# VectorE's plan and result steps reordered, and the second expert layer done one half of the rows at a time

## The chip, the cores and the metric

One core of a Trainium2 chip runs the whole kernel. The metric is device time in microseconds, the median of several executions: 927.52 us before (926.98 to 929.14).

## The reference

A gated cross-attention layer and a mixture of experts, on x of 4 x 1024 tokens of width 256:

```python
x = x + tanh(g_xattn) * attention(ctx_768, layernorm(x), ...)
xf = layernorm(x)
probs = softmax(xf @ w_router)              # 8 experts
topk_w, topk_idx = top_k(probs, 2)
h = gelu(einsum('te,ieh->tih', xf, w1) + b1)     # hidden 1024
out = einsum('tih,ihe->tie', h, w2) + b2
x = x + tanh(g_ffn) * sum(out * weights[..., None], axis=1)
```

## The kernel before

The engines' programs are written out by hand, one block each (`block.sync`, `gpsimd`, `scalar`, `vector`, `tensor`), and meet at semaphores. Up to about 479 us the kernel does the attention of the four sequences; beside it the router chooses two experts for every token, and each token's normed row, with its number and its weight, is scattered to the region of its expert in a table `routed` in memory. Behind that the expert stage runs over tiles of TM = 256 rows of one expert. Of a tile, two halves of 128 rows (m = 0, 1; MH = 2) become output partitions. Tiles 0 to 8 (KTILES = 9) belong to three experts with three tiles each, known beforehand (their first rows come from the first sequences); the last sequence's router work is done beside them. From tile 9 on, `plan_tiles` works out from the counts which rows, and which expert, each tile has; a run-time loop does these (`Fori`). In this data there are 35 tiles.

One tile goes so. SyncE loads its rows (`load_rows`, L547) into `lnf`. TensorE turns them (`turn_tile`, L1828), ScalarE and VectorE split them in a high and a low part (`turned_hi` L876, `turned_lo` L1277), since each product is done as three (high by high, low by high, high by low). TensorE does the first layer (`first_layer`, products at L1664, 48 of them, in eight chunks c of the hidden 1024), ScalarE the gelu per chunk (`hidden`, L884), VectorE the split of its outputs per pair of chunks, the quarters q = 0 to 3 (`activate`, L1302 and L1304, semaphore `g_ready`). TensorE turns the next tile's rows between its two layers, and does the second layer (`second_layer`, L1860, 48 products): for q, for m, six products into psY[m]; psY[0] is in psF, psY[1] in psO. Behind the last quarter `expert_done` is raised for each m. VectorE (`results`, L1317 to L1325) adds b2, takes the token numbers (`token_i`), multiplies by the tokens' weights, and raises `result_ready`; GpSimd (`add_rows`, L694) adds both halves to the output in memory by indirect DMAs, whose landing is `added`. `move_meta` (L1309) and `take_meta` (L1281) carry numbers and weights of the tile along.

When the next tile has another expert, VectorE cuts w1 (L1286, after ScalarE's L872, in `change_first`) behind `take_meta`, does `results`, copies b2 (`new_bias`, L1295) and cuts w2. The cut of w1 raises `w1_ready`, for which SyncE waits before it loads the next expert's w1 and, behind it in its queue, the rows of the tile after the next. When the expert stays, `keep_expert` raises `w1_ready` and `w2_ready` without work; TensorE's first layer waits for it.

The order of VectorE at the end of a tile is: four times `activate`, `move_meta`, `turned_lo` of the next tile, `take_meta`, then `keep_expert` and `results`. Three tiles have more: in tile 3 `router_logits` of the last sequence and in tile 4 its `router_slots` stand ahead of `keep_expert`, in tile 6 `plan_tiles`:

```python
else:
    if t == 6:
        plan_tiles()
    keep_expert()
    results(t)
```

SyncE loads the rows of tile 9 once all scatters have landed and the plan is there. GpSimd's queue at this place holds the adds of tile 4, six scatters, the adds of tile 5, six scatters, the adds of tile 6, four scatters, the adds of tile 7.

## Time and profile before

| | |
|---|---|
| median of 3 runs | 927.52 us |
| the profiled execution | 927.44 us, of which 925.5 us are the span |
| TensorE products busy | 857.1 us, 93% |
| VectorE busy | 645.4 us, 70% |
| ScalarE busy | 514.2 us, 56% |
| GpSimd busy | 332.1 us, 36% |
| granted TensorE clock | 0.9 or more in all 40 slices but two at 0.8 |
| chain that ended last | TensorE 55%, issue 14%, VectorE 11%, GpSimd 10% |

Times are from the start of the span. PE is TensorE's products, PEld its loads of weights (the stationary operand), DVE VectorE, ACT ScalarE, POOL GpSimd, and SPq the queue of SyncE, which issues DMAs. A row of the order of time gives start, duration, engine, line, operation and tiles, and in brackets how long the engine was idle before and what ended that. Of TensorE's products the ends are modelled and overlap the next one's start; their rhythm is told by the starts.

### The profile page before, as it was taken

To read this page: it belongs to the slowest core of one execution; us is meant where nothing else is said; L and a number is where in the kernel's file an instruction comes from. 1 tells how busy PE (TensorE), PEld (TensorE's weight loads), DVE (VectorE), ACT (ScalarE), POOL (GpSimd) and SP (SyncE) were. 2 spreads that over 40 slices of the span, in tenths; PEclk is the share of its full clock that TensorE was granted. 3 is DMA by queue.
4 is the path that set the end of the run, shared out by engine and by line. 5 is a ranking of instruction groups with operands and counts; after the bars stand their busy time and mean duration, and the time that the engine had idled before them with its cause. 6 is when DMAs were issued, how large, how long until landed. Compare 5 with 4: busy or idle time off the path is not lost.

```text
span 925.5 us, 19447 instructions
## 1 busy us (share of the span) xinstructions
PE 857.1 (93%) x5968; PEld 657.7 (71%) x5968; DVE 645.4 (70%) x1500; ACT 514.2 (56%) x1371; POOL 332.1 (36%) x241
## 2 busy tenths in 40 slices
PE   3898899999999999998989999899999999999995
PEld 3654445544455454554449999899999999999995
DVE  6767766677766767667786778675765776575685
ACT  2668775787766877558742645243433443353462
POOL 2333223332376323662153227532232223232233
PEclk9999999999999999999999999899999999999998
DMA  4801000120012201120034449352343526352272
GB/s 125 242 1 49 1 1 1 46 94 1 2 58 80 92 1 46 58 92 1 1 109 116 114 105 268 82 138 45 74 107 47 136 37 150 46 140 47 34 221 31
DMA packets 71899, 70.31 MB, mean 76 GB/s; under 512 B 18593, under 2 KB 66977, under 8 KB 71841
## 3 DMA queue, kind: packets, MB, share of 16 engines
q1 hardware_dynamic: 57696, 52.73, 19.2%
q0 software_dynamic: 13152, 16.86, 10.5%
q8 instruction: 30, 0.49, 0.2%
q14 instruction: 29, 0.23, 0.1%
q10 hardware_dynamic: 992, 0.00, 0.1%
HBM read 44.04 MB, written 26.31 MB: 76 GB/s over the span
## 4 chain that ended last, share of the span: by engine, by line
PE 55%; issue 14%; DVE 11%; POOL 10%; ACT 5%; DMA 3%; DVEq 0%; POOLq 0%; SPq 0%; ACTq 0%
PE psS L1664 22%; PE psF L1860 10%; PE psO L1860 10%; POOL rr L676 6%; PE psO L1797 4%; POOL routed L686 4%; PE psS L1781 3%; DVE p_sum L1134 3%; PE psF L1664 2%; DMA out<-V,token_i 2%; PE psF L1828 2%; ACT sq L823 1%; ACT p_ring L867 1%; DMA xr<-in_x 1%; DVE qkd L1108 1%
## 5 line engine op out<-in xcount | busy, mean ns | idle before, releaser
L884 ACT ACTIVATE V<-psS,b_col 128x256 f32<-128x256 f32 x280 | 117.1, 471 | 216.2 <-PE psS L1664 205.4
L694 POOL DMA_INDIRECT out<-V,token_i x70 | 120.4, 1720 | 271.8 <-DVE V L1325 246.4
L676 POOL TENSOR_TENSOR rr<-ssm,minus_half 128x4 f32<-128x4 f32 (+1 forms) x72 | 119.9, 1665 | 254.3 <-DVE ssm L1098 254.1
L867 ACT ACTIVATE p_ring<-psS,shift 128x1024 f32<-128x1024 f32 x128 | 136.5, 1112 | 71.9 <-PE psS L1781 71.6
L1797 PE MATMUL psO<-p_ring,V 128*64 128x512 f32 x576 | 148.5, 612 | 1.5 <-ACT o_sb L855 1.5
L1134 DVE TENSOR_TENSOR p_sum<-p_sum,p_ring 128x1024 f32<-128x1024 f32 (+1 forms) x112 | 136.0, 1215 | 0.6
L1860 PE MATMUL psF<-ln_hi,K 128*128 128x256 f32 x560 | 123.3, 284 | 0.2 <-DVE K L1304 0.2
L1781 PE MATMUL psS<-Q,K 64*128 64x512 f32 x864 | 120.2, 409 | 0.6 <-ACT p_ring L867 0.5
L1860 PE MATMUL psO<-ln_hi,K 128*128 128x256 f32 x560 | 120.2, 278 | 0.0
L1781 PEld LDWEIGHTS psS<-Q,K 64*128 64x128 f32 x864 | 75.9, 184 | 61.0 <-issue 42.7
L1304 DVE TENSOR_TENSOR K<-V,K 128x512 fp32r<-128x512 f32 x140 | 97.1, 694 | 4.8
L1302 DVE CAST K<-V 128x512 fp32r<-128x512 f32 x140 | 60.2, 430 | 51.7 <-ACT V L884 51.3
L1860 PEld LDWEIGHTS psF<-ln_hi,K 128*128 128x128 f32 x560 | 95.1, 188 | 0.8 <-issue 0.4
L1860 PEld LDWEIGHTS psO<-ln_hi,K 128*128 128x128 f32 x560 | 95.0, 188 | 0.0
L1664 PE MATMUL psS<-w_hi 128*128 128x256 f32 x280 | 81.2, 290 | 8.2 <-issue 8.2
L1664 PE MATMUL psS<-w_lo,w_hi 128*128 128x256 f32 x280 | 80.7, 288 | 0.0
L1664 PE MATMUL psS<-w_hi,w_lo 128*128 128x256 f32 x280 | 80.6, 288 | 0.0
L1664 PE MATMUL psS<-w_hi,wc_hi 128*128 128x256 f32 x280 | 79.3, 283 | 0.0
L1664 PE MATMUL psS<-w_lo,wc_hi 128*128 128x256 f32 x280 | 79.2, 283 | 0.0
L1664 PE MATMUL psS<-w_hi,wc_lo 128*128 128x256 f32 x280 | 79.2, 283 | 0.0
L1860 PE MATMUL psO<-ln_lo,K 128*128 128x256 f32 x280 | 78.0, 278 | 0.5 <-issue 0.5
L1860 PE MATMUL psF<-ln_lo,K 128*128 128x256 f32 x280 | 77.9, 278 | 0.0
(289 smaller groups left out, 1764.0 us busy)
## 6 DMA issues: line engine op xcount, KB each, us to landing
xr<-in_L_ffn_w SPq DMA_DIRECT2D x11, 1024.0 KB, 7.9
xn<-in_L_ffn_w SPq DMA_DIRECT2D x11, 1024.0 KB, 5.3
lnf<-routed SPq DMA_DIRECT2D x35, 258.0 KB
routed<-pad_rows SPq DMA_DIRECT2D x17, 258.0 KB, 9.5
xr<-in_x SPq DMA_DIRECT2D x8, 512.0 KB, 4.4
xb<-in_x SPq DMA_DIRECT2D x4, 1024.0 KB, 5.9
out<-xb SPq DMA_DIRECT2D x4, 1024.0 KB
b_raw<-in_L_ffn_b SPq DMA_DIRECT2D x11, 128.0 KB, 3.4
```

Of the source, the lines that this page charges most:

```text
L676: pool.tensor_tensor(rr[0:p, c % 2, n], ssm[0:p, c % 2, n], minus_half[0:p, n], ALU.pow).then_inc(rr_ready, 1)
L686: pool.indirect_dma_start(routed, bass.IndirectOffsetOnAxis(ap=slot_i[:, k, t:t + 1], axis=0), rows_of(b)[k][:, t, :], None, bounds_check= ...
L694: pool.indirect_dma_start(out_rows, bass.IndirectOffsetOnAxis(ap=token_i[:, m:m + 1], axis=0), y_out[:, m, :], None, bounds_check=NTOK - 1 ...
L867: act.activation(p_ring[0:p, u % RING, :], psS[u % 2][0:p].rearrange("p a n -> p (a n)"), ACT.Exp, bias=bias).then_inc(exp_done, 1)
L884: act.activation(g32[:, q % 2, (c % 2) * TM:(c % 2 + 1) * TM], psH[q][:, (c % 2) * TM:(c % 2 + 1) * TM], ACT.Gelu_apprx_tanh, bias=b1_col[ ...
L1134: dve.tensor_tensor(total, p_ring[0:p, (u - 1) % RING, :] if k == 1 else total, p_ring[0:p, u % RING, :], ALU.add).then_inc(p_added, 1)
L1302: dve.tensor_copy(g_hi[:, 2 * q:2 * q + 2, :], g).then_inc(g_hi_ready, 1)
L1304: dve.tensor_tensor(g_lo[:, 2 * q:2 * q + 2, :], g, g_hi[:, 2 * q:2 * q + 2, :].bitcast(F32), ALU.subtract).then_inc(g_ready, 1)
L1664: ins = pe.matmul(o, l, r, start=(n == 0), stop=(n == len(parts) - 1))
L1781: ins = pe.matmul(psS[u % 2][:, odd, :], kk[rows_of, f, keys], qq[rows_of, f, cols], start=(m == 0), stop=(m == len(products) - 1))
L1797: ins = pe.matmul(psO[0][head, :], V[:, (w % 2) * KT + kt, head], p_ring[:, u % RING, odd * HALF:(odd + 1) * HALF], start=(kt == 0), stop= ...
L1860: ins = pe.matmul(psY[m][:, 0:D], l[:, c, cols], r[:, c, :], start=(c == 0 and n == 0), stop=(c == HC - 1 and n == 2))
```

## The change

The second layer goes over m first and q second, so that psY[0] is complete half-way, and the wait for `g_ready` of each quarter stands in the first half alone. `results` is one operation per half, product by weight plus `y_bias`, and raises `result_ready` for each half; `y_bias`, b2 by the tokens' weights, is made in `move_meta`, two multiplications. The wait for `added` and `token_i` stand ahead of the first half. `add_rows` waits for each half by itself. `keep_expert` goes ahead of `router_logits` (tile 3) and `router_slots` (tile 4). `plan_tiles` falls into four: `plan_ends` ahead of tile 6's results but behind `keep_expert`, `plan_rows` behind them, `plan_experts` ahead of tile 7's `move_meta`, `plan_switches` ahead of tile 7's results. The steps of the plan themselves stay as they are. `late` (the turning of the last logits) goes to the second half, behind q = 2.

```diff
                 def add_rows(t):
-                    pool.wait_ge(result_ready, t + 1)
-                    pool.sem_inc(passed, 1)
                     for m in range(MH):
+                        pool.wait_ge(result_ready, t * MH + (MH + 1 + m))
+                        pool.sem_inc(passed, 1)
                         pool.indirect_dma_start(out_rows, bass.IndirectOffsetOnAxis(ap=token_i[:, m:m + 1], axis=0), y_out[:, m, :],
...
                     dve.wait_ge(meta_moved, t + 1)
                     dve.sem_inc(passed, 1)
+                    for m in range(MH):
+                        ins = dve.tensor_scalar(y_bias[:, m, :], b2_row[:], meta_now[:, m, 1:2], None, ALU.mult)
+                    ins.then_inc(bias_scaled, 1)
 
                 def results(t, first=False):
 
-                    for m in range(MH):
-                        dve.wait_ge(expert_done, t * MH + (m + 1))
-                        ins = dve.tensor_tensor(y1[:, m, :], psY[m][:, 0:D], b2_row[:], ALU.add)
-                    ins.then_inc(expert_read, 1)
                     if not first:
                         dve.wait_ge(added, t * 32)
                         dve.sem_inc(passed, 1)
                     dve.tensor_copy(token_i[:], meta_now[:, :, 0])
-                    dve.wait_ge(expert_read, t + 2)
+                    dve.wait_ge(bias_scaled, t + 1)
                     for m in range(MH):
-                        ins = dve.tensor_scalar(y_out[:, m, :], y1[:, m, :], meta_now[:, m, 1:2], None, ALU.mult)
-                    ins.then_inc(result_ready, 1)
+                        dve.wait_ge(expert_done, t * MH + (m + 1))
+                        dve.scalar_tensor_tensor(out=y_out[:, m, :], in0=psY[m][:, 0:D], scalar=meta_now[:, m, 1:2], in1=y_bias[:, m, :],
+                                                 op0=ALU.mult, op1=ALU.add).then_inc(result_ready, 1)
...
                 take_meta(4)
+                keep_expert()
                 router_logits(B - 1)
-                keep_expert()
                 results(3)
...
                 take_meta(5)
+                keep_expert()
                 router_slots(B - 1)
                 wait_bank_read(dve, ("ranks", B - 1))
                 dve.tensor_copy(pad_at[:], base[:]).then_inc(pads_known, 1)
-                keep_expert()
                 results(4)
 
                 for t in range(5, KTILES):
                     for q in range(NQ):
                         activate(t, q)
+                    if t == 7:
+                        plan_experts()
                     move_meta(t)
...
                     else:
+                        keep_expert()
                         if t == 6:
-                            plan_tiles()
-                        keep_expert()
+                            plan_ends()
+                        if t == 7:
+                            plan_switches()
                         results(t)
+                        if t == 6:
+                            plan_rows()
...
                 def second_layer(t, late=None):
-                    pe.wait_ge(expert_read, t + 1)
-                    for q in range(NQ):
-                        if q % (NQ // 2) == 0:
-                            pe.wait_ge(w2_ready, t * 2 + (q // (NQ // 2) + 1))
-                        pe.wait_ge(g_ready, t * NQ + (q + 1 + NQ))
-                        for m in range(MH):
...
+                    pe.wait_ge(result_ready, t * MH + MH)
+                    for m, q in itertools.product(range(MH), range(NQ)):
+                        if m == 0:
+                            if q % (NQ // 2) == 0:
+                                pe.wait_ge(w2_ready, t * 2 + (q // (NQ // 2) + 1))
+                            pe.wait_ge(g_ready, t * NQ + (q + 1 + NQ))
+                        cols = slice(m * P, (m + 1) * P)
+                        for c in (2 * q, 2 * q + 1):
```

## Rows read from the trace of the kernel before

**Rows 1.** The chain that ended last: start us, us, what.
```profile
577.81 4.80 issue
582.61 7.92 PE psS L1664 x48
...
655.23 5.76 PE psS L1664 x48
```

**Rows 2.** Busy time by stretch: PE, PEld, DVE, ACT, POOL, PEclk, DMA share, GB/s.
```profile
582.60:584.00 1.40, 1.39 (x6) 1.40 (x7) 1.38 (x6) 0.00 (x0) 0.00 (x0) 0.50 0.26 94
```

**Rows 3.** Order of time, VectorE, two steps of the plan in tile 6.
```profile
575.54 0.16 DVE L1352 TENSOR_TENSOR count<-base,rest 128x5 f32<-128x5 f32 x1
...
580.11 0.43 DVE L1368 TENSOR_REDUCE expert_f<-p_sum 128x39 f32<-128x273 f32 x1
```

**Rows 4.** Order of time, TensorE, start of tile 5's first layer.
```profile
554.06 0.19 PEld L1664 LDWEIGHTS psS<-w_hi 128*128 128x128 f32 x1 [1.22 <-issue]
```

**Rows 5.** Order of time, GpSimd to tile 9's transposes; last, the page's issues.
```profile
584.98 1.56 POOL L694 DMA_INDIRECT out<-V,token_i  x1 [2.76 <-DVE V L1325]
...
596.39 0.39 SPq L547 DMA_DIRECT2D lnf<-routed  x1
...
602.00 0.60 PE L1828 MATMUL psF<-ident,lnf 128*128 128x128 f32 x4
...
xr<-in_x SPq DMA_DIRECT2D x8, 512.0 KB, 4.4
```

**Rows 6.** Order of time at the switch behind tile 13; last, SyncE's waits.
```profile
667.46 0.62 DVE L1325 TENSOR_SCALAR V<-V,meta_now 128x256 f32<-128x256 f32 x2
...
668.57 0.37 SPq L547 DMA_DIRECT2D lnf<-routed  x1
...
672.63 0.42 PEld L1828 LDWEIGHTS psF<-ident,lnf 128*128 128x128 f32 x4 [0.22 <-DMA lnf<-routed]
...
SPq L565 <- DVE wc_lo L1286: 60.7, 6, 11.5
```

**Rows 7.** Order of time in the last tile: its second layer's start, and its end.
```profile
909.12 0.69 DVE L1304 TENSOR_TENSOR K<-V,K 128x512 fp32r<-128x512 f32 x1
...
909.86 0.19 PEld L1860 LDWEIGHTS psF<-ln_hi,K 128*128 128x128 f32 x1 [0.41 <-DVE K L1304]
...
915.61 0.42 DVE L1317 TENSOR_TENSOR V<-psO,b_row 128x256 f32<-128x256 f32 x1 [0.26 <-PE psO L1860]
...
919.41 1.55 POOL L694 DMA_INDIRECT out<-V,token_i  x1 [0.30 <-issue]
```

**Rows 8.** Order of time, tile 13: first and 19th weight load, last quarter.
```profile
661.15 0.19 PEld L1860 LDWEIGHTS psF<-ln_hi,K 128*128 128x128 f32 x1
...
662.44 0.69 DVE L1304 TENSOR_TENSOR K<-V,K 128x512 fp32r<-128x512 f32 x1
...
663.20 0.19 PEld L1860 LDWEIGHTS psO<-ln_hi,K 128*128 128x128 f32 x1
```

**Rows 9.** The same of tiles 0, 1 and 4.
```profile
490.80 0.19 PEld L1860 LDWEIGHTS psO<-ln_hi,K 128*128 128x128 f32 x1
491.18 0.74 DVE L1304 TENSOR_TENSOR K<-V,K 128x512 fp32r<-128x512 f32 x1
...
493.34 0.19 PEld L1860 LDWEIGHTS psO<-ln_lo,K 128*128 128x128 f32 x1 [0.65 <-issue]
...
510.19 0.19 PEld L1860 LDWEIGHTS psO<-ln_hi,K 128*128 128x128 f32 x1
...
510.76 0.69 DVE L1304 TENSOR_TENSOR K<-V,K 128x512 fp32r<-128x512 f32 x1
...
548.90 0.19 PEld L1860 LDWEIGHTS psO<-ln_hi,K 128*128 128x128 f32 x1
...
549.87 0.69 DVE L1304 TENSOR_TENSOR K<-V,K 128x512 fp32r<-128x512 f32 x1
```

**Rows 10.** Groups of instructions, VectorE, with shapes: count, busy us, mean ns.
```profile
L1172 DVE SCALAR_TENSOR_TENSOR xb<-psS,gate,xb 128x256 f32<-128x256 f32 x6 | 2.6, 479 | 2.4 <-PE psS L1664 2.4
```

More of the change, by code:

```diff
@@ L4 @@
+import itertools
 from contextlib import ExitStack
@@ L225, in flamingo_gated_layer @@
             g32 = flat(V)[:, 0:4 * TM].rearrange("p (a n) -> p a n", a=2)
-            y1, y_out = (flat(V)[:, 4 * TM + k * MH * D:4 * TM + (k + 1) * MH * D].rearrange("p (m d) -> p m d", m=MH) for k in range(2))
+            y_bias, y_out = (flat(V)[:, 4 * TM + k * MH * D:4 * TM + (k + 1) * MH * D].rearrange("p (m d) -> p m d", m=MH) for k in range(2))
             begun, jumped = (p_sum[:, k, 0:REST * NE].rearrange("p (t e) -> p t e", e=NE) for k in range(2))
@@ L326, in flamingo_gated_layer @@
             expert_done = sem("expert_done")
-            expert_read = sem("expert_read")
+            bias_scaled = sem("bias_scaled")
             result_ready = sem("result_ready")
@@ L1014, in _ @@
                 dve.sem_inc(g_ready, NQ)
-                dve.sem_inc(expert_read, 1)
+                dve.sem_inc(result_ready, MH)
                 def norm_stats(b, part):
@@ L1337, in finish, with then_plan, plan_ends @@
                         results(t)
-                def plan_tiles():
-                    plan_step = [0]
-                    def then_plan(ins):
-                        plan_step[0] += 1
-                        ins.then_inc(plan_step_done, 1)
-                        dve.wait_ge(plan_step_done, plan_step[0])
-                    wide_t = lambda a: a.unsqueeze(1).to_broadcast([P, REST, NE])
-                    wide_e = lambda a: a.unsqueeze(2).to_broadcast([P, REST, NE])
-                    at = slice(KTILES, NTILES)
+                plan_step = [0]
+                def then_plan(ins):
+                    plan_step[0] += 1
+                    ins.then_inc(plan_step_done, 1)
+                    dve.wait_ge(plan_step_done, plan_step[0])
+                wide_t = lambda a: a.unsqueeze(1).to_broadcast([P, REST, NE])
+                wide_e = lambda a: a.unsqueeze(2).to_broadcast([P, REST, NE])
+                rest = slice(KTILES, NTILES)
+                def plan_ends():
                     dve.tensor_tensor(count[:, 0:NE - KE], base[:, KE:NE], rest0[:, KE:NE], ALU.subtract)
@@ L1360, in plan_tiles, with plan_rows @@
                         then_plan(dve.tensor_tensor(ends[:, e:e + 1], ends[:, e - 1:e], needed[:, e:e + 1], ALU.add))
+                def plan_rows():
                     then_plan(dve.tensor_tensor(begun, wide_e(tile_id[:]), wide_t(ends[:]), ALU.is_ge))
@@ L1366, in plan_tiles, with plan_experts @@
                                                        op1=ALU.add))
-                    dve.tensor_scalar(tile_row[:, at], row_f[:], float(KEPT * TM), None, ALU.add).then_inc(plan_ready, 1)
+                    dve.tensor_scalar(tile_row[:, rest], row_f[:], float(KEPT * TM), None, ALU.add).then_inc(plan_ready, 1)
+                def plan_experts():
                     dve.tensor_reduce(expert_f[:], begun[:, :, 0:NE - 1], AX, ALU.add)
@@ L1850, in second_layer @@
                 def second_layer(t, late=None):
[L1851 to L1864 removed]
+                    pe.wait_ge(result_ready, t * MH + MH)
[6 more added lines that the diff above has]
+                        for c in (2 * q, 2 * q + 1):
+                            for n, (l, r) in enumerate(((g_hi, w2_hi), (g_hi, w2_lo), (g_lo, w2_hi))):
+                                ins = pe.matmul(psY[m][:, 0:D], l[:, c, cols], r[:, c, :], start=(c == 0 and n == 0),
+                                                stop=(c == HC - 1 and n == 2))
+                        if q == NQ - 1:
+                            ins.then_inc(expert_done, 1)
+                        if late and m == MH - 1 and q == NQ - 2:
                             late()
```

13 lines of the change are left out of this document (3 added, 10 removed).

## The prediction

> **What bounds the kernel now.** I read the page's busy table and slices first, then the chain of work that ended last, then the order of time around each place where the chain is not TensorE, and last the waits of SyncE. TensorE is busy for 93% of the span. The diff touches only the expert stage, 479 to 925 us of the trace: 35 tiles of 256 rows, numbered 0 to 34, each one first layer (48 products at 0.12 us, 5.76 us in all), four transposes of the next tile (0.36 us) and one second layer (48 products at 0.114 to 0.118 us). In the chain the first layers follow each other at 11.6 to 11.9 us, each 5.76 long [rows 1], so a VectorE step costs nothing there unless it makes TensorE wait. Five kinds of place matter.
>
> First, ahead of tile 7's first layer TensorE stands still for 4.80 us, and the layer then takes 7.92 us where the others take 5.76 [rows 1]; the granted clock is 0.50 at its start, the lower level of 1.2 GHz [rows 2]. The idle time costs 4.80 + 2.16 = 6.96 us. The cause is `plan_tiles`: it runs on VectorE from 575.54 to 582.6, and `keep_expert`, which lets tile 7 begin, stands behind it [rows 3]. Second, ahead of tile 5 it waits 1.22 us, with `keep_expert` behind `router_slots` [rows 4]. Third, tile 9's rows: GpSimd's queue of scatters and adds must be through before SyncE loads them [rows 5]. Fourth, switches of the expert: w1's cut on VectorE releases SyncE, which issues w1's load and behind it the rows' load, and the transposes wait for these rows [rows 6]. Fifth, the tail: two adds of GpSimd behind the last result [rows 7].
>
> **The change part by part.**
>
> *Second layer by halves.* The last quarter (q = 3) of the gelu outputs was wanted by the 37th product, it is now wanted by the 19th, some 2.1 us earlier. In the steady state the 19th weight load starts at 663.20, 2.05 us after the first (0.114 each), and VectorE ends the last quarter at 662.44 + 0.69 = 663.13 [rows 8]; the release of a weight load by VectorE takes 0.05 us (the first quarter of tile 34 ends at 909.12 + 0.69 = 909.81, the load starts at 909.86) [rows 7]. So the wait just fits, with 0.02 to 0.09 us to spare in some 25 tiles (fast tiles like 13 are the tight ones). I take 0.5 us in all; the bounds are 0 and 0.15 us for each of 25, 3.8 us. In three tiles it does not fit, for VectorE has other work between the quarters. Tile 0: ready at 491.92, wanted at 490.80, 1.2 us; but before there is a gap of 0.65 us at 493.34 that no semaphore explains, and a wait ahead of it can absorb it, so I take 0.5 (0.5 to 1.2). Tile 1: 511.45 against 510.19, 1.3 us. Tile 4: 550.56 against 548.90, and with later router logits 0.1 more, 1.8 us [rows 9]. Sum 3.6 us by the end of tile 4. Tile 6 loses 0.65 in the same way, off the path as shown below.
>
> *keep_expert ahead of router_slots* gives back the 1.2 us ahead of tile 5 [rows 4]; tile 5 begins 3.6 - 1.2 = 2.4 later than before.
>
> *The plan in four pieces.* Ahead of tile 7 nothing but the tile's own rows is left. plan_ends and plan_rows take 580.11 - 575.54 = 4.6, experts and switches 582.6 - 580.11 = 2.5 us [rows 3]. plan_ends and plan_rows stand before tile 7's first activation, which comes about 0.7 us late and catches up by the third quarter; plan_experts stands before `turned_lo(8)`, which needs 1.85 us and has some 3. All are covered. TensorE alone would then be at 2.4 + 0.65 - 6.96 = 3.9 us earlier at the end of tile 8's first layer.
>
> *What is late next: GpSimd.* Its add of tile 4 follows `router_slots`, now 3.6 us later, but the result of the first half is ready 0.8 us sooner after it (one operation where four stood): 2.8 later. From there GpSimd is busy without a pause until the add of tile 6, for which it waited 2.76 us; that wait goes, 0.3 of handover stays [rows 5]. So the last scatter and the load of tile 9's rows (596.39 before) are 0.35 later, 596.74. Such a load takes at most 4.1 us (with a w1 load in front, below); one of twice its bytes lands in 4.4 [rows 5], half of which is 2.2, an estimate. Nothing stands in front of it here: I take 2.7, bounds 2.2 and 4.1. The transposes, at 602.00 before, then begin at 596.74 + 2.7 + 0.1 = 599.5: **-2.5 us** (-3.0 to -1.1). Of the 7 us at tile 7 the larger part is thus not seen, and TensorE waits about 1.4 us there.
>
> That an idle of this size leaves the clock up is what [rows 4] show, 1.22 us at the full level. The Trainium skill (TensorE: Matmul & The Clock Gate, What's actually happening) says that the throttled state is the default and activity releases it; the trace agrees at tile 7 (0.50 after 4.80 us idle). By that rule alone the removed idle time is worth more than its length, which the sum already has from the rows.
>
> *y_bias.* Two multiplications per tile stand ahead of `turned_lo`; the same operation on the same shapes is x2 in 0.62, one begins 0.265 after the other [rows 6]: 0.53 us. In tiles without a switch they lie beside the second layer. At a switch VectorE runs without a break from the last quarter to w1's cut, so w1_ready, w1's load, the rows' load and the next tile's transposes all come 0.53 us later. SyncE waited for this cut 6 times, and the transposes stood waiting for the rows (load issued 668.57, released 672.63) [rows 6]. Six of the seven switches in the loop load rows behind w1; the four at tiles 13, 18, 21, 26 cost 4 x 0.53 = **+2.1 us**. At 31, 32 and 33, one tile each, VectorE is itself the chain: 0.67 for the rows (0.53 and 0.14 more from the cut of w2), 0.6 at tile 33 and 0.35 at tile 34 for the last quarters: **+1.6 us**. Bounds for both together 0 and 4.5.
>
> *results.* It removes two additions and two multiplications (about 1.3 us after the last product) and puts two scalar_tensor_tensor at 0.48 each, about 0.40 in a row [rows 10]. Off the path except behind the last tile. The wait for `added` now stands before the first half's result: queued behind it are only the second half's result and the next activation, and the adds of the tile before have landed by then. SyncE's queue keeps its order; GpSimd's wait is per half.
>
> *Tail.* The second add began 919.41 - 915.61 = 3.80 us after the last addition of VectorE began [rows 7]. The first add lasts 1.55 and hands over in 0.30, so it began 1.95 after that row, of which four operations took 0.34 + 0.12 + 0.62 = 1.08 and the handover to GpSimd 0.87. Now the first half's add is done earlier, and the second starts 0.44 + 0.87 = 1.3 after VectorE begins: **-2.5 us**.
>
> The sum: -2.5 + 2.1 + 1.6 + 0.5 - 2.5 = -0.8. The profiled execution took 927.44 us, its span being 925.5, within 0.1 us of the median 927.52. Forecast **926.7**.
>
> **The rivals.** A measurement of this kernel tells apart about 0.2%, that is 1.9 us; unchanged is 925.7 to 929.4.
>
> *The thin wait breaks the stream (slower).* If the wait for the last quarter, met only 0.02 to 0.09 us ahead, delays the load of weights beside the running product, each steady tile loses 0.15 us instead of 0.02. For it: where the release was late, the following product came 0.1 us later than the rhythm [rows 7]. Against it: in these tiles the release is before the load's own start [rows 8]. It decides from about 0.1 us per tile: 25 x 0.13 = 3.3, time 930.0. The Trainium skill (TensorE: Matmul & The Clock Gate, Step-by-step: what each phase is for) says that weight loads are pulled ahead of products in flight; a wait in front of one would forbid that for this load, and the time would be this rival's.
>
> *The switches cost nothing (faster).* If w1's load and the rows do not come later, because the landing is set by other transfers, 2.1 and 0.7 go: 923.9. For it: the visible wait was only 0.22 us of idle each [rows 6]. Against it: SyncE named the cut each time.
>
> *The plan's full 7 us come through (faster).* If GpSimd's chain is shorter (the early waits absorbed, adds quicker), tile 9 is 3.9 earlier instead of 2.5, and with less at the switches: 921.5 to 924.
>
> *The change does not do what it says.* If tile 7's first layer stays held by the shortened plan (a wait of VectorE that the trace doesn't show), the clock falls again and 2.5 us are lost: 929.5 or more.
>
> The pace of the second layers, 0.114 or 0.118 us, changes from tile to tile without visible cause and moves the sum by 1.5 us either way in each case.
>
> **How the numbers follow.** Forecast 0.42, thin wait 0.22, free switches 0.20, full gain 0.12, not as said 0.04. The predicted time is the first one's, whose own range is 925 to 928.5. The range reaches from the middle of the full gain to just over the thin wait: 923.0 to 930.6. Faster by over 0.2%: 0.20 + 0.12 and a tenth of the forecast's case, less some pace, 0.34; slower: most of the thin wait and of the last, 0.23; between, 0.43.
>
> **What would show it.** Tile 7's first layer should take 5.8 us at clock 1.00 right behind tile 6. Waits for VectorE in the second layers of tiles 0, 1, 4 and 6 of 0.5 to 1.8 us. Transposes of tile 9 waiting for `lnf<-routed` at about 598 to 599.5. Idle before the transposes behind a switch of 0.7 instead of 0.22 us. The last add 2.5 us closer to the last product. I would be wrong if the second layers grew longer in every tile, if the row loads behind switches did not move, or if TensorE did not wait before tile 9.

## The result and the profile after

The changed kernel takes 931.91 us (median of 15 runs, 929.20 to 936.74), the kernel before beside it 927.66 us (926.38 to 929.53, 15 runs): ratio 1.0051, 95% interval 1.0039 to 1.0064. It is 4.3 us slower; the forecast was 926.7 with a range up to 930.6. The profiled execution took 931.64 us, its span 929.9. Of the runs further down one single execution (quarters in tiles 0 to 8) took 2632.87 us; it is left out of its ratio. Lines of kernel.py are shifted by the change: first layer L1680, second layer L1876, transposes L1844, gelu L885, splits L1303 and L1305, y_bias L1314, token_i L1322, results L1326, adds L695.

What of the change went as forecast is seen first. The waits for the last quarter, TensorE's loads of weights in the second layers of tiles 0, 1 and 4 (order of time; they answer [rows 9]; the row at 549.35 is the wait for the third quarter of tile 4):

```profile
490.43 0.19 PEld L1876 LDWEIGHTS psF<-ln_hi,K 128*128 128x128 f32 x1 [1.42 <-issue]
...
510.49 0.19 PEld L1876 LDWEIGHTS psF<-ln_hi,K 128*128 128x128 f32 x1 [1.25 <-DVE K L1305]
...
549.35 0.19 PEld L1876 LDWEIGHTS psF<-ln_hi,K 128*128 128x128 f32 x1 [0.79 <-issue]
...
551.10 0.19 PEld L1876 LDWEIGHTS psF<-ln_hi,K 128*128 128x128 f32 x1 [0.99 <-DVE K L1305]
```

In the steady tile 13 the last quarter is ready at 665.58 + 0.69 = 666.27, and the load that wants it is the second of the row at 666.23, which has no idle time in front of it and starts some 0.07 us later, at 666.34 ([rows 8] before):

```profile
665.58 0.69 DVE L1305 TENSOR_TENSOR K<-V,K 128x512 fp32r<-128x512 f32 x1
...
666.23 0.30 PEld L1876 LDWEIGHTS psF<-ln_hi,K 128*128 128x128 f32 x2
```

The chain of work that ended last shows the loss. It answers [rows 1]: start, us, what.

```profile
573.95 2.83 PE psF L1876 x24
576.78 2.83 PE psO L1876 x24
579.61 4.79 PE psS L1680 x40
586.84 1.50 PE psS L1680 x4
590.55 2.28 another core or an unknown queue
595.91 2.83 PE psO L1876 x24
598.74 5.77 PE psS L1680 x48
```

Tile 7's first layer now begins at once behind tile 6's second layer, 579.61, and 40 of its products run in 4.79 us at full pace. The 4.80 us of idle time and the slow layer of [rows 1] are gone. But then the tile falls apart: it lasts from 579.6 to 598.7, 19.1 us, where an undisturbed one takes 11.7. ScalarE's gelus of this tile (order of time, ScalarE):

```profile
585.42 0.84 ACT L885 ACTIVATE V<-psS,b_col 128x256 f32<-128x256 f32 x2 [10.83 <-PE psS L1680]
588.37 0.84 ACT L885 ACTIVATE V<-psS,b_col 128x256 f32<-128x256 f32 x2 [2.11 <-PE psS L1680]
589.90 0.84 ACT L885 ACTIVATE V<-psS,b_col 128x256 f32<-128x256 f32 x2 [0.69 <-remote]
592.86 0.84 ACT L885 ACTIVATE V<-psS,b_col 128x256 f32<-128x256 f32 x2 [2.12 <-remote]
```

The first pair of gelus needs the first twelve products. By the records these end at 581.05 (the last begins at 580.76), yet the gelu begins at 585.42, 4.4 us later. The other pairs begin 5.9, 6.0 and 4.9 us behind the recorded end of their products. It isn't ScalarE: the trace also has the moments at which the semaphore `h_done` rises, which TensorE raises per chunk, and they are 585.40, 588.35, 589.88 and 592.84, each 0.02 us ahead of a gelu. So the signal of a finished chunk comes late. I call these late signals; whether the product itself finishes late (the ends of products are modelled) or only its signal, the trace doesn't tell. TensorE itself stops twice in the middle of a chunk, where the code has no wait, its clock falls, and its second layer waits for quarters. A late fetch of instructions isn't seen: the one instruction packet in this stretch (580.37) took 0.94 us, and 1.08 us in a trace without late signals. A window of the stretch (us, PE, PEld, DVE, ACT, POOL busy, PEclk, DMA share, GB/s), then TensorE's loads:

```profile
587.00:590.00 3.00, 3.00 (x14) 2.76 (x14) 1.17 (x3) 0.94 (x3) 2.39 (x3) 0.51 0.63 79
```

```profile
585.35 0.19 PEld L1680 LDWEIGHTS psS<-w_lo,wc_hi 128*128 128x128 f32 x1 [1.16 <-issue]
...
586.83 0.19 PEld L1680 LDWEIGHTS psS<-w_hi,wc_lo 128*128 128x128 f32 x1 [0.93 <-issue]
...
590.55 0.19 PEld L1876 LDWEIGHTS psF<-ln_hi,K 128*128 128x128 f32 x1 [0.78 <-issue]
592.04 0.19 PEld L1876 LDWEIGHTS psF<-ln_hi,K 128*128 128x128 f32 x1 [0.72 <-issue]
...
594.93 0.19 PEld L1876 LDWEIGHTS psF<-ln_hi,K 128*128 128x128 f32 x1 [2.12 <-DVE K L1305]
```

The tail (order of time, VectorE and GpSimd) answers the last rows of [rows 7]:

```profile
918.53 0.17 DVE L1322 CAST token_i<-meta_now 128x2 int32<-128x2 f32 x1 [1.08 <-issue]
918.66 0.48 DVE L1326 SCALAR_TENSOR_TENSOR V<-psF,meta_now,V 128x256 f32<-128x256 f32 x1
920.09 1.54 POOL L695 DMA_INDIRECT out<-V,token_i  x1 [6.25 <-DVE V L1326]
920.50 0.48 DVE L1326 SCALAR_TENSOR_TENSOR V<-psO,meta_now,V 128x256 f32<-128x256 f32 x1 [1.35 <-PE psO L1876]
921.94 1.55 POOL L695 DMA_INDIRECT out<-V,token_i  x1 [0.30 <-issue]
```

The last load of weights of the second layer is at 915.19 before and at 920.07 now. The second add begins 4.22 us behind it before, 1.87 us now: 2.35 us closer, as forecast. But from the add's start to the end of the span it is 6.1 us before (919.41 to 925.5) and 8.0 us now (921.94 to 929.9).

I had to explain two things: the late signals, and the end that didn't follow the adds.

### The profile page after: what moved, and what is told of

Read it like the earlier page. It is cut to its first block, busy times and chain, and to the rows that moved or that the text cites. A ratio compares the mean times of both kernels' runs of the same rounds, so it can differ in the third digit from the quotient of the medians.

```text
span 929.9 us, 19517 instructions
## 1 busy us (share of the span) xinstructions
PE 857.9 (92%) x5968; PEld 655.9 (71%) x5968; DVE 648.3 (70%) x1500; ACT 514.1 (55%) x1371; POOL 331.3 (36%) x241
## 3 DMA queue, kind: packets, MB, share of 16 engines
q1 hardware_dynamic: 57696, 52.73, 19.2%
## 4 chain that ended last, share of the span: by engine, by line
PE 45%; issue 16%; DVE 15%; POOL 10%; ACT 5%; DMA 4%; SPq 2%; DVEq 1%; another core or an unknown queue 0%; ACTq 0%; POOLq 0%
PE psS L1680 15%; PE psO L1876 8%; PE psF L1876 7%; POOL rr L677 6%; PE psO L1813 4%; POOL routed L687 3%; PE psS L1797 3%; DMA lnf<-routed 3%; DVE p_sum L1135 3%; PE psF L1680 2%; ACT sq L824 1%; PE psF L1844 1%; ACT p_ring L868 1%; DVE K L1303 1%; DVE K L1305 1%
## 5 line engine op out<-in xcount | busy, mean ns | idle before, releaser
L885 ACT ACTIVATE V<-psS,b_col 128x256 f32<-128x256 f32 x280 | 116.9, 470 | 219.9 <-PE psS L1680 205.3
L695 POOL DMA_INDIRECT out<-V,token_i x70 | 118.6, 1694 | 274.1 <-DVE V L1326 239.3
L1876 PE MATMUL psF<-ln_hi,K 128*128 128x256 f32 x560 | 109.4, 287 | 6.8 <-DVE K L1305 4.9
L1876 PE MATMUL psO<-ln_hi,K 128*128 128x256 f32 x560 | 103.7, 279 | 0.0
L1303 DVE CAST K<-V 128x512 fp32r<-128x512 f32 x140 | 60.9, 435 | 58.3 <-ACT V L885 57.9
L1305 DVE TENSOR_TENSOR K<-V,K 128x512 fp32r<-128x512 f32 x140 | 97.2, 694 | 4.8
L1876 PEld LDWEIGHTS psF<-ln_hi,K 128*128 128x128 f32 x560 | 89.0, 189 | 9.1 <-DVE K L1305 5.0
L1876 PEld LDWEIGHTS psO<-ln_hi,K 128*128 128x128 f32 x560 | 87.7, 188 | 0.0
L1680 PE MATMUL psS<-w_hi 128*128 128x256 f32 x280 | 79.6, 284 | 2.3 <-issue 2.3
L1680 PE MATMUL psS<-w_lo,wc_hi 128*128 128x256 f32 x280 | 79.5, 284 | 1.1 <-issue 1.0
L1680 PE MATMUL psS<-w_hi,wc_lo 128*128 128x256 f32 x280 | 79.5, 284 | 0.4 <-issue 0.4
L1680 PE MATMUL psS<-w_hi,wc_hi 128*128 128x256 f32 x280 | 79.5, 284 | 0.0
L1680 PE MATMUL psS<-w_hi,w_lo 128*128 128x256 f32 x280 | 79.3, 283 | 0.0
L1680 PE MATMUL psS<-w_lo,w_hi 128*128 128x256 f32 x280 | 79.2, 283 | 0.0
L1876 PE MATMUL psF<-ln_lo,K 128*128 128x256 f32 x280 | 78.3, 279 | 0.0
L1876 PE MATMUL psO<-ln_lo,K 128*128 128x256 f32 x280 | 78.0, 279 | 0.0
```

The source lines that it names most:

```text
L695: pool.indirect_dma_start(out_rows, bass.IndirectOffsetOnAxis(ap=token_i[:, m:m + 1], axis=0), y_out[:, m, :], None, bounds_check=NTOK - 1 ...
L885: act.activation(g32[:, q % 2, (c % 2) * TM:(c % 2 + 1) * TM], psH[q][:, (c % 2) * TM:(c % 2 + 1) * TM], ACT.Gelu_apprx_tanh, bias=b1_col[ ...
L1303: dve.tensor_copy(g_hi[:, 2 * q:2 * q + 2, :], g).then_inc(g_hi_ready, 1)
L1305: dve.tensor_tensor(g_lo[:, 2 * q:2 * q + 2, :], g, g_hi[:, 2 * q:2 * q + 2, :].bitcast(F32), ALU.subtract).then_inc(g_ready, 1)
L1680: ins = pe.matmul(o, l, r, start=(n == 0), stop=(n == len(parts) - 1))
L1876: ins = pe.matmul(psY[m][:, 0:D], l[:, c, cols], r[:, c, :], start=(c == 0 and n == 0), stop=(c == HC - 1 and n == 2))
```

## The experiments

The runs fell on several chips. The kernels of one group ran on one chip and are compared with the kernel before on that chip; a comparison across groups is across chips, and is called so.

**First group, one chip: the two parts alone.** The order alone puts into the kernel before this and the four pieces of the plan:

```diff
                 take_meta(4)
+                keep_expert()
                 router_logits(B - 1)
-                keep_expert()
                 results(3)
```

> Only the order of VectorE is changed (keep_expert ahead of router_logits and router_slots, the plan in four pieces); the second layer, results and add_rows are those of before. In the changed kernel's trace the semaphore of the first layer's chunks (h_done) rises in tile 7 at 582.50, 585.40, 587.59, 588.35, 589.11, 589.88, 591.37 and 592.84 us: 10.3 us for seven chunks where an undisturbed tile takes 7 x 0.72 = 5.0. Theory A (tile 7, begun right behind tile 6, is stretched by something that tile 7 of before missed because it stood still for 4.8 us): the stretch shows here too, tile 7's first layer takes over 8 us, and the time is 926 to 929 us, within 0.2% of before. Theory B (the stretch comes from the second layer by halves, or from VectorE's new results): tile 7's first layer takes 5.8 to 6 us here, and the time is 921 to 924 us.

The halves alone keep the order of before:

```diff
+                    pe.wait_ge(result_ready, t * MH + MH)
+                    for m, q in itertools.product(range(MH), range(NQ)):
```

> Only the second layer by halves with its results, y_bias and add_rows per half; the plan and keep_expert stand where they stood before, so tile 7 waits for the whole plan. Theory A: tile 7's first layer takes 7.9 us at the lower clock after 4 to 5 us of idle, as before; the waits for the last quarter in tiles 0, 1 and 4 (2.9 us in the changed kernel's trace) and the switches put the time at 929 to 932 us. Theory B: the same idle and the same slow layer, but with more lost behind it, over 933 us.

One line of the kernel before moved:

```diff
                     else:
+                        keep_expert()
                         if t == 6:
                             plan_tiles()
-                        keep_expert()
                         results(t)
```

> The kernel before with one line moved: in tile 6 keep_expert stands ahead of the undivided plan, the results of tile 6 stay behind it. Tile 7's first layer is then free at once, with no piece of the plan on its path. Theory A: the layer is stretched to 8 to 12 us, time 926 to 930. Theory B: it takes 5.8 us; but its activations stand behind 7 us of plan and 1.7 us of results, so the second layer begins some 2 us late; the clock stays up: 922 to 925 us.

And the changed kernel unchanged:

> The changed kernel itself, a second look, since its 15 runs spread from 929.2 to 936.7 us where those of before spread from 926.4 to 929.5. Theory A: tile 7's first layer is stretched again (its chunk semaphores take over 8 us), though not by the same amount, and the median is 930 to 934. If the stretch was an accident of the one profiled execution, the layer takes 5.8 us in this profile while the median stays near 932, and the loss has to be looked for elsewhere.

Measured (before 927.49): order alone 924.02, ratio 0.9960 (0.9946 to 0.9973); halves alone 934.44, 1.0064 (1.0051 to 1.0078); one line 929.39, 1.0017 (1.0006 to 1.0027); changed kernel 932.27, 1.0048 (1.0034 to 1.0062). By the ratios the order brings 3.7 us, and the halves cost 5.9 alone and 8.2 on top of the order. Neither theory fits whole. The late signals are in every trace of this chip. In the order alone the first pair of gelus of tile 7 comes 4.6 us late, yet the tile takes 14.7 us and the kernel is faster (my 926 to 929 was wrong):

```profile
583.07 0.84 ACT L884 ACTIVATE V<-psS,b_col 128x256 f32<-128x256 f32 x2 [9.38 <-remote]
```

In the halves alone tile 7 begins after the idle time, and its gelus are on time; the late signals (2.2 to 3.9 us) lie in tile 6, which takes 19.2 us against 16.8 before. The time, over 933 us, is theory B's.

The moved line shows the other limit, the one the prediction had named. Its chain of work that ended last, then TensorE's load and the window:

```profile
592.41 4.33 DMA routed<-p_ring,slot_i
597.52 3.56 DMA lnf<-routed
601.13 1.11 PE psF L1828 x4
```

```profile
601.13 0.71 PEld L1828 LDWEIGHTS psF<-ident,lnf 128*128 128x128 f32 x4 [4.92 <-DMA lnf<-routed]
```

```profile
598.00:602.00 4.00, 0.87 (x5) 0.87 (x5) 1.52 (x4) 0.00 (x0) 0.00 (x0) 0.59 0.54 99
```

Tile 7 begins at once and takes 12.9 us, with gelus 1.1 to 2.6 us late, but tile 6's results stand behind the undivided plan, GpSimd's adds and scatters stand behind them, tile 9's rows come late, TensorE waits 4.92 us and the clock falls: tile 8 takes 18.8 us. The gain of tile 7 is given back one and a half tiles later. Theory A's time (926 to 930) came true, but not by its mechanism. In the order alone the plan is divided, and tile 8 takes 11.7 us.

**Second group, another chip: where the halves cost.**

```diff
-                    for m, q in itertools.product(range(MH), range(NQ)):
+                    turns = itertools.product(range(MH), range(NQ)) if halves else [(m, q) for q in range(NQ) for m in range(MH)]
+                    for m, q in turns:
```

> The changed kernel with the second layer by quarters again in the first nine tiles (0 to 8), by halves only in the run-time loops; results, y_bias and the order of VectorE stay as changed. The order alone measured 0.9960 of before, the halves alone 1.0064, both together 1.0048. Theory C (the halves cost only in the first nine tiles: the early wait for the last quarter in tiles 0, 1 and 4, and in tiles 5 to 7 where TensorE's chunk signals come up to 6 us late and the second layer by halves can wait less for them): the time falls by 6 us or more against the changed kernel, to 923.5 to 926. Theory D (the halves cost in the loops, at the switches and in the steady tiles): the time stays over 928.

The pads (`pad(e)` for eight experts) moved in SyncE's program from ahead of `load_rows(7, ...)` to behind `load_b1(3)`:

> The changed kernel with the eight pad stores (2.1 MB) behind the loads of tiles 7 and 8 in SyncE's queue instead of ahead of tile 7's rows. Theory E (the chunk signals of tiles 6 and 7 come late because the DMA engines are saturated by pads, scatters and weight loads at once, share 1.0 or more from 560 to 582 us): tile 6's transposes of tile 7 no longer wait 0.86 us for rows, signals of tile 6 come on time, and those of tile 7 are late only if the pads now lie beside it; the time changes by more than 2 us, either way. Theory F (the signals are late for the scatters that GpSimd issues one behind the other, whatever else is moved): tile 7's signals stay 4 to 6 us late, the time stays within 2 us of the changed kernel's.

The multiplications of y_bias moved from `move_meta` to the start of `results`:

> The changed kernel with the two multiplications of y_bias moved from move_meta to the start of results, behind the cut of w1. The prediction put their place at 0.53 us for each of four switches and 1.6 us at switches 31 to 33. If that holds, the cut of w1 and the next rows come 0.5 us earlier at each switch and the time falls by 1.5 to 3.7 us; the traces of before and after moved apart by only 0.1, 0.2, 0.8 and 0 us at these switches, by which the time falls by 0.5 to 1.2 us. The tail gets 0.3 us longer at most, if the multiplications stand behind the last product, and nothing if they don't.

> All three edits together: quarters in tiles 0 to 8, pads behind the loads of tiles 7 and 8, y_bias behind the cut of w1. By theory C the time is 922 to 925 us, below before and below the order alone (924.0) by the shorter tail (1 to 2 us). By theory D it stays over 927.

Measured (before 927.98): quarters in tiles 0 to 8 928.45, 0.9999 (0.9984 to 1.0014); pads last 937.00, 1.0090 (1.0077 to 1.0103); y_bias later 931.06, 1.0036 (1.0023 to 1.0049); all three 929.22, 1.0011 (1.0002 to 1.0020). The changed kernel itself didn't run on this chip. Against its 1.0048 of the first group the quarters bring some 4.5 us (2.6 to 6.4, an estimate from the two intervals): theory C has the place right for most of its 6 us, though 928 was the bound above which I would have believed theory D. The y_bias edit gives 1.1 us by the same comparison (1.0036 against 1.0048), but these two intervals overlap. The traces of this one chip say more. TensorE's waits for rows ahead of the transposes in tiles 9 to 33, in the kernel with quarters in tiles 0 to 8, then with y_bias later (its waits: line, what ended them, us in all, times, longest):

```profile
PEld psF L1844 <- DMA lnf<-routed: 4.8, 6, 1.3
...
PEld psF L1844 <- DMA lnf<-routed: 1.1, 4, 0.3
```

With pads last they are 4.4 us, with all three edits 1.0. These tiles together take 299.4 and 298.9 us with y_bias in `move_meta`, 297.5 and 297.4 with it behind the cut: 1.4 to 2.0 us. The last tile and the end take 21.9 and 22.5 us with the edit, 22.0 and 21.4 without, so a part is given back there. The gain lies between the two forecasts, and neither is settled.

Pads beside tile 7 made it worse. Their kernel's chain and ScalarE:

```profile
581.89 4.08 PE psS L1680 x34
594.00 2.54 issue
```

```profile
591.97 0.84 ACT L885 ACTIVATE V<-psS,b_col 128x256 f32<-128x256 f32 x2 [14.96 <-PE psS L1680]
```

Here the first gelus of tile 7 come 8.6 us behind their products and the tile takes 23.4 us; with all three edits, again with the pads there, they come 6.9 us late and it takes 19.2. With the pads in their old place they come 0.8 us late (quarters in tiles 0 to 8) and 3.3 us (y_bias later), and the tile takes 16.5 and 14.5. So on this chip the lateness goes with the traffic beside the tile, by two profiles each, in favour of theory E. The combined kernel, forecast at 922 to 925, took 929.22; tile 7 alone is 7 us over an undisturbed one.

**Third group, another chip: pads out of the way, and the tail.** The pads go behind the load of tile 9's rows, with the changed kernel and with the order alone; and the loops of all five engines are cut (VectorE's line):

```diff
-                with dve.Fori(SURE - 1, NTILES) as t, dve.If(t < tiles):
+                with dve.Fori(SURE - 1, 40) as t, dve.If(t < tiles):
```

> The changed kernel with the eight pad stores behind the load of tile 9's rows, where in this data they still come in time for the tiles that read them; from 557 to 592 us they are gone. With them beside tile 7 (last run) the chunk signals of tile 7 came 8.6 to 10.9 us late, with them at 557 to 567 us 4.4 to 6.0 us late. Theory E (the pads' traffic makes the signals late): the gelus of tiles 6 and 7 start within 1 us of the recorded end of their products, tile 7's pitch falls from 19.1 to under 14 us, and the time falls by 4 us or more, to 924 to 928; tiles 8 or 9, which now lie beside the pads, may get late signals. Theory F (the scatters or the weight loads do it): tile 7's signals stay over 3 us late and the time stays over 930.

> The order alone (0.9960 of before) with the pad stores behind the load of tile 9's rows. There the signals of tiles 6 and 7 came 2.5 to 4.6 us late, and the two tiles took 13.3 and 14.8 us where an undisturbed one takes 11.7. Theory E: both take under 12.3 us, and the time falls by 2 to 4 us, to 920 to 922. Theory F: no change, 923 to 925.

> The changed kernel with the run-time loops bounded at 40 turns of the tile number instead of 48: 8 empty turns fewer behind the 35 tiles of this data, nothing else. In the traces the second add of the last tile lands at 923.17 us before and the program ends at 925.47; changed, it lands at 925.73 and ends at 929.89. Theory G (the end is set by VectorE, which goes through the 13 empty turns at 0.68 us each behind its last result, so that the gain of the last adds isn't seen): the time falls by 3.5 to 4 us, the end comes 0.4 us behind the landing. Theory H (the end is set by something in the landing): it falls by less than 1 us.

> The kernel before with the same loops bounded at 40. Theory G: the empty turns stand only 1.9 us beyond the landing of the last add here, so the time falls by 1.7 to 2 us, to about 925.8; the distance to the changed kernel with short loops is then 2 us smaller than that between the two kernels as they are. Theory H: it falls by less than 0.5 us.

Measured (before 925.96): pads behind tile 9's rows 931.68, 1.0058 (1.0036 to 1.0080); the same with the order alone 921.96, 0.9960 (0.9946 to 0.9974); changed kernel with short loops 923.43, 0.9976 (0.9967 to 0.9986); kernel before with short loops 924.00, 0.9978 (0.9966 to 0.9990).

The pads' runs seemed to prove theory E: tiles 6 and 7 took 11.9 and 11.6 us. They don't, because the changed kernel with short loops, whose pads lie where they lay, had no late signals either. On this chip there were none. Nor did it help: tiles 8 and 9 took 14.6 and 14.4 us, since tile 9's and 10's rows came late. The time of 924 to 928 for the first of them was a miss. The order alone has the same ratio with the pads moved as without (0.9960 on both chips), so in no ratio did a moved pad show a gain.

The tail is settled. The short loops save the kernel before 2.0 us, as theory G said, and the changed one 3.4 us, a little under the 3.5 to 4 forecast (926.85 on the same chip in the last group, 923.43 here). As they are the two lie 1.1 us apart on this chip, with short loops the changed one is 0.6 us ahead, which is inside the intervals. The last rows of the chains (short loops changed, short loops before), whose spans end at 920.7 and 922.5:

```profile
916.61 1.55 POOL out L695
```

```profile
918.42 1.55 POOL out L694
```

From the last add's start to the end it is now 4.1 us in both, where it was 8.0 and 6.1. By the traces the last add lands 0.4 us ahead of the end in both, where that distance was 4.2 us in the changed kernel and 2.3 us before. The records of the loops' branch instructions, which the page doesn't count as busy, show VectorE going through the turns from 35 to 47 at 0.68 us each, until 929.55 in the changed kernel and 925.14 before; GpSimd is through at 929.20, TensorE at 927.93. So VectorE is through 9.95 us behind the last load of weights before and 9.48 us behind it now, 0.5 us closer. The gain of 2.35 us for the adds was real and hidden.

**Fourth group, another chip: control, pads again, and the parts with short loops.**

> The changed kernel once more, as the control for the next run on the same chip. In the last group of runs no kernel showed late chunk signals in tiles 6 and 7, not even the changed kernel with short loops, whose pads lie where they lay; in the eight profiles ahead of it that could show them, seven did. Theory J (the late signals belong to the chip or the moment, not to the pads): the two runs of this group agree with each other, either both with late signals or both without; without them the ratio to before is 1.001 to 1.003. Theory E (pads): this one shows 3 to 6 us of lateness in tile 7 and a ratio of 1.004 to 1.006.

> The changed kernel with the pad stores behind the load of tile 9's rows, beside its control. Theory E: tiles 6 and 7 take under 12 us each, where the control takes 12.7 and 17 to 19 us. Theory J: as late as the control, if that is late. In both, tiles 8 and 9 take 14.5 us each as in the last run, since tile 9's and tile 10's rows now come late; the time is not below the control's by more than 3 us.

> The order of VectorE as changed, results as changed with y_bias behind the cut of w1, the second layer by quarters up to tile 15 and by halves from tile 16 on, loops bounded at 40 turns. Order alone is worth 3.7 us (0.9960), the 8 empty turns 2.0 us without the halves in the tail and 3.9 us with them (landing at 0.4 us before the end in both). If the halves cost nothing in tiles 16 to 33 the time is 0.4 to 2 us below the next run's; if the rows behind switches 18, 21, 26 and 31 come late for them (0.2 to 1.2 us each so far) it is equal to it or above.

> The order alone with loops bounded at 40 turns; second layer and results as before. 0.9960 and 0.9978 together: ratio 0.9938, about 921.9 us where before takes 927.6.

Measured (before 925.59): the changed kernel 925.50, ratio 1.0002 (0.9992 to 1.0012); pads behind tile 9's rows 930.05, 1.0045 (1.0028 to 1.0062); order, halves from tile 16 on, short loops 918.54, 0.9928 (0.9916 to 0.9940); order alone with short loops 918.97, 0.9937 (0.9924 to 0.9950).

The same changed kernel is 0.5% slower than before on one sort of chip and equal on this one. Theory J is right in that. With the pads moved tile 8 takes 18.6 us, tile 9 11.8 us (I had expected 14.5 each), against 13.3 and 11.8 in the control: the two tiles lose 5.3 us by the late rows, more than the 4.5 us of the whole. The control's ScalarE in tile 7 (first gelu 0.04 us behind its products), TensorE's wait at tile 9's transposes, and the waits of SyncE's queue:

```profile
583.61 0.84 ACT L885 ACTIVATE V<-psS,b_col 128x256 f32<-128x256 f32 x2 [6.49 <-PE psS L1680]
585.05 0.84 ACT L885 ACTIVATE V<-psS,b_col 128x256 f32<-128x256 f32 x2 [0.60 <-PE psS L1680]
...
601.20 0.42 PEld L1844 LDWEIGHTS psF<-ident,lnf 128*128 128x128 f32 x4 [1.68 <-DMA lnf<-routed]
```

```profile
SPq L610 <- DVE tile_next L1388: 13.9, 1, 13.9
...
SPq L611 <- DMA routed<-p_ring,slot_i: 2.3, 1, 2.3
```

The sum of the two parts, 0.9960 and 0.9978, gives 0.9938; measured 0.9937. The halves from tile 16 on, with the shorter tail, bring no more than 0.4 us over that, inside the intervals. Both are the fastest versions found; they beat before by 6 to 7 us, but a bound of 40 is safe only where no data can need more tiles, so the order alone (0.9960) is the one to keep as it stands.

**Last group: control and pads once more,** for a chip with late signals.

> The changed kernel as the control of the next run. So far all ten profiles of the first three chips (the kernel before, the changed one and its variants) had late chunk signals in tile 6 or 7, and all eight of the last two chips had none; the changed kernel's ratio to before was 1.005 on the former and 1.000 on the latter. Theory J: this profile falls into one of the two sorts, ratio 1.004 to 1.006 with tile 7 over 14 us, or 0.999 to 1.002 with tile 7 under 12 us.

> The pad stores behind the load of tile 9's rows. If the control has late signals: theory E (on such a chip the pads' traffic makes them late) expects none in tiles 6 and 7 here, both under 12.1 us; theory F (scatters and weight loads do) expects 3 us or more of lateness in tile 7. If the control has none, neither is told apart, and tiles 6 and 7 take 11.6 to 12.1 us as in the two looks before.

Measured (before 925.74): control 926.85, 1.0011 (0.9996 to 1.0026); pads moved 931.38, 1.0061 (1.0044 to 1.0077). The chip was one without late signals (the third group's), so the pads stay open.

All traces together: on three chips, or at three times, ten of ten profiles have late signals in tile 6 or 7 (over 1 us), and the kernel before takes 927.5 to 928.0 us; in the other three groups, on two chips, none of ten has, and it takes 925.6 to 926.0. TensorE's stops in the middle of a chunk, seen in six profiles, are all in the first ten. One more thing divides the same twenty profiles without exception: in the first ten, 68 to 109 of the 3,234 or 3,303 rises of semaphores are missing from the trace, on every engine but GpSimd; in the others at most one is. Whether the recording of a trace has a part in the late signals is an open question that no run here touches.

## Why the prediction was wrong, point by point

The stages, from the traces (start of a tile's first layer to that of a later one; us), against the terms of the sum. "Late" is the chip of the result, changed less before. "Not late" is the control of the fourth group less the kernel before with short loops, its tail less that of before. Each cell is one profile against one.

```
stage                  forecast   not late   late
start of the stage         0        +0.9     -0.4
tiles 0 to 4             +2.4       +2.1     +1.3
tiles 5 to 8             -4.9       -3.3     +1.2
tiles 9 to 33            +4.2       +0.7     +2.6
tile 34 and the end      -2.5       -0.3     -0.3
sum                      -0.8       +0.1     +4.4
```

*The step that failed* is "Tile 7's first layer should take 5.8 us at clock 1.00 right behind tile 6", with the plan's pieces "All are covered". It begins there, but on the chip of the result its signals come 4.4 to 6.0 us late. Tiles 5 to 8 took 1.2 us more than before where 4.9 us less were forecast. Those 6.1 us are more than the whole miss of 5.2 us; 4.5 of them are lost only where signals are late (+1.2 against -3.3). Before was spared: its idle time ahead of tile 7 [rows 1] stood where the signals would have been late, and its gelus of tile 7 begin on time; where signals are late it takes 1.0 us more in these tiles (54.0 against 53.0 us), the order alone 2.7 (51.5 against 48.7), the changed kernel 5.5 and 4.0 (55.2 and 53.7 against 49.7). A second layer by quarters wants the last quarter at its 37th product, one by halves at its 19th, so late gelus reach TensorE 2.1 us sooner.

The order brings 0.40% on either sort of chip (0.9960; 0.9937 against 0.9978), and the halves cost 0.9% on one and 0.4% on the other. The late gelus explain only a part of that difference. On top of the order alone the changed kernel loses 3.7, 2.3 and 4.5 us in tiles 0 to 4, 5 to 8 and 9 to 33 in the traces of the first group, and 4.7, 1.2 and 0.4 us without late signals (both with short loops). Tiles 5 to 8 make 1.1 us of the difference, the tiles from 9 on 4.1, where the transposes wait for their rows (below). No rival had this case. The trace of before held a hint of it that I didn't read: in tile 6 the second pair of gelus begins 1.53 us behind the end of its products, 0.04 us in the traces without late signals.

*The early waits* were right in place: 0.2, 1.3 and 0.6 us more for tiles 0, 1 and 4 with the earlier `keep_expert` (forecast 0.5, 1.3, 0.6). For tile 0 the agreement means little, for I had overlooked its clock. TensorE has no product for 2.30 us ahead of it, and in six of the twenty profiles, before among them, the granted clock fell to its lower level in tile 0's first layer. Windows of this stretch, before, then changed:

```profile
479.95:484.40 4.45, 4.45 (x26) 4.23 (x26) 2.55 (x3) 2.12 (x3) 2.73 (x2) 0.64 0.78 244
```

```profile
479.55:484.00 4.45, 4.45 (x31) 3.50 (x32) 2.77 (x4) 2.71 (x5) 2.81 (x2) 1.00 0.74 245
```

Both kernels before that the table subtracts had the fall, neither of the two changed ones did. With halves tile 0 takes 21.1 to 21.3 us without the fall and 22.1 to 22.5 with it. By quarters it takes 19.6 to 21.4 us without. So at the same clock the halves cost tile 0 something between nothing and 1.6 us, and by this chance both columns are some 1.3 us too low in tiles 0 to 4.

*What is late next* was right, tile 9's rows, and mis-sized: their load was issued at 597.11, against 596.42 in the kernel before with short loops. Tile 0 had begun 0.9 us later there, so this is 0.2 us earlier (forecast 0.35 later; [rows 5]). The transposes waited 1.68 us (forecast 1.4), but the load took 601.20 - 597.11 = 4.1 us, my upper bound, where I took 2.7. That is 1.4 of the 1.6 us missing in this stage. On the chip of the result these rows waited 21.0 us for the last piece of the plan instead, since tile 7 had held VectorE up:

```profile
SPq L610 <- DVE tile_next L1388: 21.0, 1, 21.0
```

*y_bias and the switches* came out differently on the two sorts of chip: +4.2 forecast, +2.6 on the chip of the result, +0.7 without late signals. In tiles 9 to 33 the transposes waited 0.8 us for rows before and 3.2 us in the changed kernel (order alone 0.5, changed again 4.0); by the runs above it is the later cut of w1 that does it, as the prediction said. Without late signals the same waits are 1.6 us in the kernel before with short loops and 1.3, 1.5 and 2.6 us in the three traces of the changed kernel: there the rival "The switches cost nothing" was the better reading of [rows 6]. What sets the difference isn't shown. TensorE's waits of the changed kernel on the chip of the result, then in the control of the fourth group:

```profile
PEld psF L1844 <- DMA lnf<-routed: 3.2, 6, 0.9
...
PEld psF L1844 <- DMA lnf<-routed: 1.5, 4, 0.5
```

*The steady thin wait* costs next to nothing: 24 products of a half still take 2.73 to 2.83 us, and in tiles 9 to 33 TensorE waited once for the last quarter, 0.3 us. The rival "The thin wait breaks the stream" isn't borne out. The Trainium skill (TensorE: Matmul & The Clock Gate, Step-by-step: what each phase is for) says that weight loads are pulled ahead of products in flight; a wait met 0.07 us ahead (666.27 against 666.34 in tile 13) took nothing from the stream here.

*The tail* was right for the adds and wrong for the program: 2.35 us, of which 0.3 is seen. This term, too, failed: -2.5 forecast, -0.3 measured. I took the chain's last row, an add [rows 7], for what sets the end, and didn't ask what filled the 6.1 us from its start to the end of the span.

On a chip without late signals the sum is nearly right (+0.1 measured, -0.8 forecast; ratio 1.0002) only because errors cancel: 1.6 and 2.2 us too hopeful in tiles 5 to 8 and the tail, 0.3 and 3.5 us too fearful in tiles 0 to 4 and 9 to 33; that is luck.

## What to carry to other kernels

An idle time that is taken out may have covered a disturbance, as that ahead of tile 7 did; before it is counted as a gain, look how late the signals between engines come in the tiles around it (start of the consumer less recorded end of the producer), and give a consumer that waits earlier less credit there. Read what lies between the last useful transfer and the end of the span: run-time loops with a generous bound cost a turn for each tile that isn't there, on the engine that is through last. Where a part can be had alone, measure it alone: the order was worth 0.4%, and the halves hid it. Before one profile is subtracted from another by stage, compare their granted clocks in that stage, and compare kernels on one chip.

## What the runs showed of the hardware

On three of the chips or occasions TensorE's semaphore signals came up to 10.9 us behind the recorded ends of its products while pads, scatters, adds and weight loads were under way (between 563 and 598 us; in the changed kernel the DMA share is 0.9 to 1.2 from 560 to 582), several of them then rising 0.07 us apart; VectorE's came within 0.02 us in the same stretch where they are recorded. On the others the same kernel, with the same transfers at the same place, had none. On one chip that had it, tile 7's second pair of gelus came 5.2 and 2.6 us late with the pads in their place (quarters in tiles 0 to 8; y_bias later) and 10.9 and 6.2 us late with the pads beside the tile. Why chips or moments differ, and whether pads, scatters, loads or the recording do it, stays open. An empty turn of a run-time loop took VectorE 0.68 us. 4.92 us of idle time lowered the granted clock (0.59 in that window), 1.68 us didn't; behind the 2.30 us without a product ahead of tile 0 it fell in six of twenty profiles (0.64 over 4.45 us before, 1.00 in the changed kernel).
